# Moving the strips' DRAM-to-DRAM copies from SyncE's queue to GpSimd's in a routed depthwise convolution block

## The reference

```
x_proj = 1x1 convolution of x, 128 -> 64 channels
att1   = depthwise 3x3 or 5x5 of x_proj      (kernel chosen per sample: argmax of a linear map of the channel means)
att2   = depthwise 7x7, 9x9 or 11x11 of att1, dilation 3 (chosen in the same way from att1's means)
o      = concat(att1, att2)                  (128 channels)
maps   = [mean over channels of o, max over channels of o]
gate   = sum of the 2 channels of sigmoid(7x7 convolution of maps, 2 -> 2 channels, plus bias)
out    = o * gate + x
```

## Time and profile before

| | us |
|---|---|
| median of 3 runs | 6073.19 |
| lowest and highest of them | 6070.11 and 6082.16 |
| the profiled execution, its own time | 6065.23 |
| its span, first to last instruction | 6063.4 |

### The profile page before, as it was taken

The page is one execution under the profiler, slowest core; times in us unless marked ns, Lnnn a source line. Parts: engine busy times, 40 slices in busy tenths (PEclk is TensorE's granted clock), DMA queues, the critical chain, the costliest instruction groups (busy, mean ns, idle before and its releaser), DMA issues.

```text
span 6063.4 us, 156224 instructions
## 1 busy us (share of the span) xinstructions
PE 4839.7 (80%) x62816; PEld 3258.9 (54%) x62816; DVE 3152.8 (52%) x3931; ACT 2834.7 (47%) x5378; POOL 1053.2 (17%) x1574
## 2 busy tenths in 40 slices
PE   5678888888888888888888888788888889884453
PEld 2237464655747455474746546474654747464442
DVE  3315446454755645475564646556454755645345
ACT  3455454545545454544545544454545445451120
POOL 2001011111212111121211111121111112111322
PEclk9889898898989889898989989898898989897675
DMA  9655777878988787898878788887878888786957
GB/s 228 191 145 180 191 178 223 222 220 216 256 209 212 221 220 217 217 257 213 214 224 220 223 210 251 210 215 223 217 220 211 257 214 209 220 201 177 223 128 193
DMA packets 1033175, 1284.55 MB, mean 212 GB/s; under 512 B 670750, under 2 KB 865737, under 8 KB 1001886
## 3 DMA queue, kind: packets, MB, share of 16 engines
q1 hardware_dynamic: 899468, 723.43, 50.1%
q0 software_dynamic: 64304, 410.01, 21.4%
q10 hardware_dynamic: 69026, 146.11, 9.2%
HBM read 950.16 MB, written 456.70 MB: 232 GB/s over the span
## 4 chain that ended last, share of the span: by engine, by line
PE 52%; DMA 19%; SPq 8%; DVE 8%; issue 7%; ACT 3%; ACTq 2%; POOL 1%; DVEq 0%; POOLq 0%
PE psC L1070 19%; PE psA L1007 10%; PE psA L1008 10%; SPq L432 6%; DMA out_dram<-RX 5%; DMA RX<-in_x_dram 5%; DMA RX<-w_d 4%; PE psB L1038 4%; PE psA L943 3%; PE psB L1049 3%; PE psB L1017 2%; DVE RX L1379 2%; DMA map_d<-RX 2%; PE psB L952 1%; DVE MM L1295 1%
## 5 line engine op out<-in xcount | busy, mean ns | idle before, releaser
L1070 PE MATMUL psC<-RX 61*60 61x96 f32 (+7 forms) x49152 | 1492.2, 269 | 257.5 <-issue 112.9
L1070 PEld LDWEIGHTS psC<-RX 61*60 61x60 f32 x49152 | 1423.7, 135 | 324.4 <-issue 310.7
L860 ACT ACTIVATE L<-psC 124x120 f32 (+4 forms) x2048 | 394.8, 287 | 910.4 <-PE psC L1070 865.8
L1007 PE MATMUL psA<-X,RX 128*128 128x240 f32 x1280 | 639.9, 589 | 126.5 <-ACT RX L825 125.1
L667 POOL COPY RX<-RX 64x720 f32<-64x720 f32 x512 | 438.9, 863 | 1708.4 <-DMA RX<-w_d 1705.6
L1038 PE MATMUL psB<-ident,L 124*128 124x124 f32 x2160 | 417.7, 336 | 321.9 <-DVE RX L1379 279.0
L830 ACT ACTIVATE X<-psA,bias 128x246 f32<-128x246 f32 x1024 | 636.8, 735 | 57.2 <-issue 22.7
L1295 DVE TENSOR_REDUCE MM<-L 124x135 f32<-124x2160 f32 (+1 forms) x192 | 535.3, 2843 | 233.7 <-ACT L L860 233.7
L1008 PE MATMUL psA<-X,RX 128*128 128x240 f32 x1280 | 632.4, 583 | 0.0
L1379 DVE TENSOR_TENSOR RX<-psB,RX 128x360 f32<-128x360 f32 (+7 forms) x1200 | 366.3, 351 | 473.3 <-DMA RX<-in_x_dram 242.4
L850 ACT ACTIVATE RX<-L 128x1080 f32 (+1 forms) x256 | 543.2, 2129 | 132.3 <-DMA L<-strip_d 132.2
(11 more groups left out here) (122 smaller groups left out, 4802.6 us busy)
## 6 DMA issues: line engine op xcount, KB each, us to landing
RX<-in_x_dram POOLq DMA_DIRECT2D x48, 2560.0 KB, 18.6
RX<-w_d ACTq DMA_DIRECT2D x512, 180.0 KB, 4.2
RX<-in_x_dram SPq DMA_DIRECT2D x128, 720.0 KB, 10.1
out_dram<-RX SPq DMA_DIRECT2D x128, 720.0 KB, 10.3
nat_d<-X SPq DMA_DIRECT2D x320, 280.0 KB
L<-strip_d SPq DMA_DIRECT2D x192, 405.0 KB, 12.4
strip_d<-nat_d SPq DMA_DIRECT2D x48, 1440.0 KB
RX<-nat_d POOLq DMA_DIRECT2D x130, 400.0 KB, 6.5
```

Of the source, the lines that this page charges most:

```text
L860: ins = nc.scalar.activation(dst[:, 0:NU2 - par, 15 * r:15 * r + nq, par, :], src[:, par:BR:2, :, :], ACT.Identity)
L1007: nc.tensor.matmul(o[:, :, 0:T1], w[:, ch, 96:224], rhs, start=True, stop=False, skip_group_check=True)
L1070: ins = nc.tensor.matmul(o[:, :, 0:kk, a:b], w2t[2 * q + p][rows, ch, z:z + PB], src[rows, 2 * p + ch, 0:nf, 3 * cg + dc:3 * cg + dc + kk, ...
```

## The change

The function `make_strips` moves from SyncE's program to GpSimd's, unchanged in what it copies. SyncE called it at the end of turn `s` for sample `s`. GpSimd calls it in turn `s + 1` for the same sample (`k`), behind the load of band 5 of x and ahead of `begin1`. It has one more wait, for the stores of att1 (`att1_stored`), which SyncE had waited for earlier in its own order. The wait in SyncE for `strip_stored` ahead of `land` stays.

```diff
@@ sync @@
-            def make_strips(s):
-                wait_alone(sp, landed, LND * s)
-                if isinstance(s, int) and s == 0:
-                    sp.wait_ge(s_zeroed, 16 * NZ)
-                for p in range(3):
-                    for p0, n in row_groups(p):
...
-                            sp.dma_start(bass.AP(strip_d.tensor, d0 + do, [[1920, n]] + mid + [[1, run]]),
-                                         bass.AP(nat_d.tensor, f0 + fo, [[3 * W * C2, n]] + mid2 + [[1, run]])).then_inc(strip_stored, 16)
...
                     if t.early:
                         early_pieces(m)
-                    make_strips(s)
@@ gpsimd @@
+            def make_strips(s):
+                wait_alone(pool, landed, LND * s)
+                wait_alone(pool, att1_stored, ST1 * (s + 1))
+                if isinstance(s, int) and s == 0:
+                    pool.wait_ge(s_zeroed, 16 * NZ)
...
+                            pool.dma_start(bass.AP(strip_d.tensor, d0 + do, [[1920, n]] + mid + [[1, run]]),
+                                         bass.AP(nat_d.tensor, f0 + fo, [[3 * W * C2, n]] + mid2 + [[1, run]])).then_inc(strip_stored, 16)
...
                         load_x(s, b)
+                if t.conv2:
+                    make_strips(k)
                 if isinstance(s, int) and s == 0:
                     set_ones()
                 if t.one:
```

More of the change, by code:

```diff
@@ L675, in store_map1 @@
                     pool.dma_start(map1_d[s, m, 143:163, :], v[0:20, 5, :]).then_inc(map1_stored, 16)
+            def make_strips(s):
[3 more added lines that the diff above has]
+                    pool.wait_ge(s_zeroed, 16 * NZ)
+                for p in range(3):
+                    for p0, n in row_groups(p):
+                        d0 = p * BK * 54 * 1920 + p0 * 1920
+                        f0 = s * (PIX * C2) + (p + 3 * p0) * W * C2
+                        for do, fo, strips, run in ((54 * 1920, 15 * C2, 4, 1920), (15 * C2, 0, 1, 960), (5 * 54 * 1920, 135 * C2, 1, 1600)):
+                            mid = [[54 * 1920, strips]] if strips > 1 else []
+                            mid2 = [[1920, strips]] if strips > 1 else []
+                            pool.dma_start(bass.AP(strip_d.tensor, d0 + do, [[1920, n]] + mid + [[1, run]]),
+                                         bass.AP(nat_d.tensor, f0 + fo, [[3 * W * C2, n]] + mid2 + [[1, run]])).then_inc(strip_stored, 16)
             def load_at(n, u):
```

## The result

The changed kernel takes 6151.45 us in the median of four runs (6120.28 to 6164.86), against 6072.84 for the kernel before on the same chip, four runs too. The ratio is 1.0119, with a 95% interval of 1.0095 to 1.0144: **slower by 1.2%**. The profiled execution has an own time of 6158.5 us and a span of 6156.4, 93 us above the profiled one of before.

The account below looks back on a forecast made before the run. Mostly TensorE, with waits for DMA; x bands and maps paths end within 1.4 us at L987. Turns 3 to 15 +96, turn 2 +15, turn 1 -5, turn 16 +2: +108 on 6065.2, 6173, median 6181 us; range 6015 to 6240.

Parts of the forecast that it names:

- maps stored (L438): Last map store, slowed behind band 5 and strips: landed at T+32.7, counted from T, band 3's issue.
- slower matmuls behind: First 14 matmuls of L1017 after TensorE's idle time: lower granted clock, 1.7 us charged per turn.
- 24 x 0.33 + 2.5 = 10.4: Read-back of the maps: 24 runs per engine, each behind one strips' run, 10.4 us in place of 3.0.
- The stuck stores: Map stores caught behind band 5 with strips following: one costs 3.3 us, two cost 9.2 us.
- My 4.7 for all turns: Delay of caught map stores: 4.7 us taken per turn, between one store's 3.3 and two stores' 9.2.
- 13 x 7.4: Turns 3 to 15: L987's equivalent comes 7.4 us later in each turn, 96 us in sum.
- the last step of the sum: From profiled execution to median of the runs: 8 us added, 6173 to 6181 us.
- the term for turn 16: Turn 16, without x: strips run beside the map transfers, no longer ahead of them, +2 us.
- The maps win the race: Rival: all twelve map stores land before band 5's first packets; -4 us in 13 turns, about 6020 us; chance 0.12.
- Small packets pass unhindered: Rival: short packets pass the strips freely, every turn like turn 2; -101 us, 5972 us; chance 0.09.
- The strips hold everything until they end: Rival: map transfers wait until the strips end; 12.4 us later per turn, 6250 us; chance 0.15.
- No change: Rival: the 7.4 us gained at a turn's start are given back exactly; about 6073 us; chance 0.07.

Follow-up runs that it names:

- e1: Changed kernel, with GpSimd waiting from turn 2 until the maps are read back before issuing the strips: 6057.29 us, ratio 0.9985.
- e5: Changed kernel, with GpSimd waiting from turn 2, ahead of band 5's load, until the maps' stores have landed: 6079.99 us, ratio 1.0018.
- e7: Changed kernel, with each strips' DMA copying only one row for samples 1 to 15: 5980.4 us, ratio 0.984.
- e2: Kernel before, with SyncE issuing the strips in turn s + 1 behind the read-back of the maps: 6042.63 us, ratio 0.996.
- e4: Changed kernel, with VectorE's combine moved from ahead of the sum over band 5 to behind route_means: 6102.99 us, ratio 1.0067.
- e6: Changed kernel, with GpSimd issuing the strips at the end of turn s behind store_map1, ahead of bands 3 and 4: 6300.54 us, ratio 1.0372.
- e10: Kernel before, with SyncE issuing the strips behind the maps' read-back, in runs of half the length: 6039.39 us, ratio 0.9954.
- e3: Changed kernel, with each strips' DMA cut in two, runs of half the length, same bytes: 6133.65 us, ratio 1.0093.

## Why the prediction was right, and where its sizes were off

**Direction and mechanism held.** The prediction had said: band 3 lands 9 us after issue and TensorE's wait for it goes; measured, 9.0 to 11.2 and 111.3 to 38.5 us. L432 issues in about 18 us; measured, 16 to 19. L438's DMAs take about 10 us; `combine` waits longer than 8.95 (in turn 12 it is 23.50); L987 waits over 10 us for the statistics (16.55). That L438 comes 4 us or more behind band 5's landing is so in eight of the nine lost turns (4.7 to 9.4 us; 2.7 in turn 5). e1 and e5 keep the maps clear of the strips, e7 takes the strips' bytes away, and in all three the loss is gone but for 0.2% (ratios 0.9985, 1.0018 and 0.984). So the loss is that of the strips beside and ahead of the maps, and not of their issue on GpSimd.

**In a lost turn the steps add up almost as written.**

| step | predicted | measured, turn 12 |
|---|---|---|
| maps stored (L438) | T+32.7 | T+31.6 |
| read-back | 10.4 | 13.6 |
| maps back | T+43.1 | T+45.2 |
| to L987 or L989 | 6.8 | 6.8 |
| L987 or L989 | T+49.9 | T+52.1 |
| slower matmuls behind | 1.7 | 2.9 (6.89 - 3.99) |

The step "24 x 0.33 + 2.5 = 10.4" was too small. The rest, 13.2 - 2.5 = 10.7 us for 24 runs, makes 0.45 us per run: the share of 1.5 long packets shown above, where I had read one for one. The stuck stores were well sized. By the packets of 120 and 40 B in the trace, one store was caught whole in turns 3, 5, 9, 12, 13 and 15, and L438 came 2.7 to 5.8 us behind band 5's landing (predicted 3.3 and the 0.4 of before); two were caught in turns 2, 7 and 10, 8.7 to 9.4 us (predicted 9.2 and 0.4). My 4.7 for all turns lay between.

**What failed is "13 x 7.4": not every turn is lost.** I had seen that the race was within a microsecond ("whether the last store is issued more than about 1 us ahead of band 5's issue") and even had the margin about right (the turns split between 0.24 and 0.84 us), but then took one outcome for all turns, and gave the other to a rival for all turns. The race came out differently from turn to turn. The profiled execution of +93 us, counted from the rows of each turn:

| part | predicted | measured |
|---|---|---|
| up to the start of turn 2 | -5 | -11.6 |
| turn 2, to L989 | +13 | +17.3 |
| turns 3 to 15, to L989, lost | +74 (13 turns, 5.7 each) | +59.4 (8 turns, 7.4 each) |
| the same, won | none | -14.8 (5 turns, -3.0 each; the rival had -4) |
| L989 to the first convolution, turns 2 to 15 | +24 (14 turns, 1.7 each) | +26.5 (14 turns, 1.9 each) |
| rest of turns 2 to 14 | 0 | +7.8 |
| behind turn 15's first convolution, with turns 16 and 17 | +2 | +8.4 |
| sum | +108 | +93 |

Too many lost turns are set against lost turns that were each dearer, 7.4 us at L989 instead of 5.7. In turn 16, which I had only guessed at, the maps were back 36.7 us after the issue of L423, against 26.6 before. And the last step of the sum, 8 us up from the profiled execution to the median, went the other way: the median 6151.45 is 7 us below the profiled 6158.5. That the forecast is only 30 us off is in part luck: the dearer lost turns, the term for turn 16 and the rest of the turns were short, the number of lost turns and the last step were too high.

**The slower matmuls.** I had put the slower fourteen matmuls down to TensorE's idle time ahead of them. Three windows over them, of the changed kernel (turn 12), of before (turn 8) and of e2 (turn 12): window, us, PE, PEld, DVE, ACT, POOL busy (count), granted clock, DMA share, GB/s.

```profile
4225.50:4232.50 7.00, 7.00 (x16) 3.94 (x16) 3.07 (x18) 0.00 (x0) 3.43 (x6) 0.56 0.80 182
```

```profile
2752.50:2756.50 4.00, 3.97 (x17) 2.31 (x17) 2.90 (x18) 0.00 (x0) 3.40 (x6) 1.00 0.67 167
```

```profile
4139.00:4146.00 7.00, 7.00 (x16) 3.93 (x15) 3.05 (x18) 0.00 (x0) 3.40 (x6) 0.53 0.99 296
```

The granted clock was 0.56 after 16.55 us of idle time in the first, and 1.00 after 1.38 us in the second. In turn 2 of before, whose 5.68 us the prediction reads as a lower clock, it was 0.70 (643.8 to 649.5 us), after 1.32 us. The third is 0.53 after only 1.71 us, and taken alone it would speak against my reason. It is an exception. I took the fourteen matmuls of turns 2 to 15 in all thirteen traces, 182 in all. In the 54 with the longest idle time right ahead of them (2.7 to 20.5 us, ahead of L989 or, in e4, of L1019) every one was slow, 5.6 to 7.2 us at a granted clock of 0.55 to 0.71; all fourteen of the changed kernel are among them. Of the other 128, with at most 2.3 us, 115 took 3.99 to 4.00 us at full clock and 13 were slow, five of them in the kernel before. An earlier band 3 does not do it by itself: e5 has it in every turn as the changed kernel has, its maps come early, and its matmuls took 3.99 us in all fourteen turns. So the reason agrees with the traces, and the size too (1.7 us predicted, 1.9 measured per turn). What made the 13 slow after short idle time stays open.

**The rivals.** "The maps win the race" is what 5 of 13 turns did. At L989 they gained 3.0 us each, where the rival had 4, but the slower matmuls, which it had left out, take back 2 of them. "Small packets pass unhindered" is refuted by the 13.22 us. "The strips hold everything until they end" fell for most turns: the strips flow until T+47.4 to T+50, and in turn 12 the maps were back at T+45.2. In turns 2, 7 and 10 they came at T+47.3 to T+47.9, within half a microsecond of the strips' end, so this case is nearly what the worst turns did. "No change" fell: what the move changed was beside which transfers the bytes flow. e6 has the copies in the other queue, 14.7 us later against `store_map1`, and is 228 us slower than before, 16 us per turn. Band 3 lands 31 us after the first of the copies is issued (9.9 and 21.5), against 14.6 + 15.2 = 30 before: what the strips do to it is the same. But before, those 14.6 us ran while GpSimd was still waiting for the first maps and storing them, and here band 3 comes late by them. So what counts is which work the issuing engine has behind the copies, and when it gets to them. Issuing the copies takes 9.87 us in e6's turn 12, beside an estimated 20 us of transfer (6.55 MB at the 328 GB/s of the earlier trace rows).

## What to carry to other kernels

A large DRAM-to-DRAM copy for which nothing waits can still cost time (here about 92 us in its old place, 171 us in the new one): ask which transfer stands beside or behind it in each place, above all transfers of many short runs; here each short packet met one to 1.5 long ones. Where two events come within a microsecond of each other there is a race, and its price must be reckoned as a mix of its outcomes, here none, one or two caught stores. Here a wait of 2 us that let the short transfer go first gave back most of the loss, and putting the copy right behind the short transfer, in the queue that issues both, gave the largest gain (0.4%).

## What the runs showed of the hardware

- q0 carries what GpSimd issues and q1 what SyncE issues: with the strips moved (before, after), q0 went from 410.01 to 514.90 MB and q1 from 723.43 to 618.56, and 16 samples of 6.55 MB are 104.8. q10 had 146.11 MB in both; the sizes of ScalarE's DMAs in the kernel before add up to 146.05.
- The queues share the 16 engines that the profile counts. The times of their packets add up to 95.7 + 4.3 = 100.0% of these; in the changed kernel's turn 12, 4205 to 4218 us, to 91.3% for q0 and 8.7% for q1; in e1's turn 12, 4150 to 4162 us, to 81.0% for q0, 18.0% for q10 and 3.7% for q1 (102.7 in all, since the records overlap a little). By the starts and lengths of the packets in the traces, 16.1, 16.1 and 16.3 of them were open at once on average, whichever queue they were in.
- "DMA to landing" ends where the waiting engine goes on: in turn 12 of the changed kernel L438's second DMA is issued at 4205.39 and lands 13.2 us later (the two land after 8.6 and 13.2), at 4218.61, and VectorE's L1330, idle for 23.50 us until then, starts at 4218.64.
- Two loads of 120 KB, 384 runs of 640 B (L438), took 2.4 to 2.6 us alone and 13.2 us in turn 12 of the changed kernel (13.4 at most in all its turns), beside a copy with runs of 3.8 to 7.7 KB. In the 13 us shown of turn 12, 562 long packets were served beside their 384 short ones.
- One store of 162 runs of 40 B took 12.30 us (changed kernel, turn 12) when a load of 1760 KB was issued on the other queue 0.1 us after it, with the copies behind that load; with 1.4 us between the last store and the load (turn 11), all stores had landed by SyncE's next step, 1.4 us after the last issue.
- A store with nine outer rows left nine packets of 4 B beside its data: 27 in q1 for the three stores of turn 12 between 4192 and 4205 us, beside 162 packets of 40 B and 324 of 120 B. The 18 more copies per sample of e10 against e2 left 192, as nine with 48 outer rows at 16 each and nine with 6 or 5 at one per row (48 together) would. The nine engines per store that the prediction took agree with that; which engine a packet was on, the traces don't name. For the same 18 copies GpSimd's queue had more of them, 480 per sample against SyncE's 192 (after against before).
- The strips' copies have 960 runs per sample. With the runs cut in half in the program there were 960 more data packets per sample on SyncE's queue (e10 against e2) and 80 more on GpSimd's (e3 against the changed kernel), where 640 packets of 7680 B stayed, two halves in one.
- The same fourteen matmuls took 5.6 to 7.2 us at a granted clock of 0.55 to 0.71 in all 54 turns with the longest idle time right ahead of them (2.7 to 20.5 us), of 182 turns in thirteen traces, and 3.99 to 4.00 us at full clock (1.00) in 115 of the other 128.
